# Attention-times-values product: from fp32 matmuls on half tiles to three fp32r matmuls on zero-padded full tiles

## The reference

```
x = x + 0.5 * F(layernorm(x))          # call 0
x = x + G(layernorm(x))                # middle stage, 16 heads, full attention
x = x + 0.5 * F(layernorm(x))          # call 1
```

```
h = shift_token(x)                     # second half of the features from the token before
q, k, v = split(h @ wqkv)              # 8 heads of 64
q, k = rotary(l2norm(q) * qs, l2norm(k) * ks)
o = local_attention(q, k, v)           # window 128: a block of 128 queries sees its own block and the one before
x = x + o @ wo
h = layernorm(shift_token(x)) * lg + lb
a, g = split(h @ w1 + b1)
x = x + (a * gelu(g)) @ w2 + b2
```

## Time and profile before

| | |
|---|---|
| median of 3 runs | 4246.81 us (4245.44 to 4254.26) |
| the profiled execution | 4246.81 us, span 4245.1 us |
| matmul engine busy | 3828.6 us, 90% |
| VectorE, ScalarE, GpSimd busy | 62%, 53%, 52% |
| call 0, middle stage, call 1 (roughly) | 44 to 1415, 1415 to 2790, 2790 to 4215 us |
| granted matmul clock, mean | 0.958 |

### The profile page before, as it was taken

The page is one execution under the profiler, slowest core; times in us unless marked ns, Lnnn a source line. Parts: engine busy times, 40 slices in busy tenths (PEclk is TensorE's granted clock), DMA queues, the critical chain, the costliest instruction groups (busy, mean ns, idle before and its releaser), DMA issues.

```text
span 4245.1 us, 75747 instructions
## 1 busy us (share of the span) xinstructions
PE 3828.6 (90%) x23552; PEld 3152.1 (74%) x23552; DVE 2628.4 (62%) x7288; ACT 2252.1 (53%) x5232; POOL 2197.2 (52%) x2175
## 2 busy tenths in 40 slices
PE   4898999899998879999999999968999998989987
PEld 3777777677777668888888888857777777777776
DVE  5666666666677455555555565546666665666764
ACT  2555665556655445454444544535556555566554
POOL 3455455545555345655555555635545554545652
PEclk9899999999999989999999999989999998999999
DMA  4000001110001010000000000010100011100000
GB/s 133 15 24 30 17 17 38 47 32 32 22 22 35 23 45 16 11 16 11 7 16 17 1 16 31 6 38 15 36 17 17 17 52 42 34 23 23 32 30 23
DMA packets 119072, 114.75 MB, mean 27 GB/s; under 512 B 13181, under 2 KB 116233, under 8 KB 118793
## 3 DMA queue, kind: packets, MB, share of 16 engines
q1 hardware_dynamic: 118792, 111.44, 8.1%
HBM read 73.69 MB, written 29.36 MB: 24 GB/s over the span
## 4 chain that ended last, share of the span: by engine, by line
PE 61%; DVE 15%; issue 9%; POOL 6%; ACT 5%; DMA 2%; SPq 1%; DVEq 0%; POOLq 0%; ACTq 0%
PE psum L1248 15%; PE psum L1249 14%; PE psum L1250 14%; PE psum L1350 5%; DVE probs L970 3%; PE psum L1360 3%; PE psum L1462 2%; ACT probs L713 2%; PE psum L1374 2%; PE psum L1339 2%; DVE nrm L1024 1%; POOL ge_lo L617 1%; PE psum L1392 1%; POOL probs L580 1%; PE psum L1442 1%
## 5 line engine op out<-in xcount | busy, mean ns | idle before, releaser
L617 POOL TENSOR_TENSOR ge_lo<-ge,ge_hi 128x512 fp32r<-128x512 f32 x512 | 722.7, 1415 | 527.9 <-DVE ge_hi L1137 283.1
L580 POOL TENSOR_SCALAR probs<-probs,rz 128x256 f32<-128x256 f32 (+1 forms) x1024 | 457.8, 466 | 653.7 <-DVE rz L984 653.7
L713 ACT ACTIVATE probs<-probs,nb,rq 128x256 f32<-128x256 f32 (+1 forms) x1024 | 575.8, 564 | 108.9 <-DVE nb L978 108.1
L801 ACT ACTIVATE ge<-psum 128x512 f32<-128x512 f32 x512 | 306.8, 599 | 611.8 <-PE psum L1462 579.1
L1137 DVE CAST ge_hi<-ge 128x512 fp32r<-128x512 f32 x512 | 249.3, 488 | 533.0 <-ACT ge L801 526.8
L970 DVE CUSTOM_DVE_ANT_0 probs<-psum,mask 128x256 f32<-128x256 f32 (+1 forms) x1024 | 339.5, 387 | 317.8 <-PE psum L1350 201.1
L570 POOL TENSOR_TENSOR rinv<-ssq,minus_half 128x16 f32<-128x16 f32 x128 | 377.0, 2946 | 119.5 <-DVE ssq L947 113.0
L1248 PE MATMUL psum<-wqkv_hi,hT_hi 128*128 128x512 f32 x768 | 341.7, 445 | 21.7 <-DVE turned_sin L936 15.2
L590 POOL TENSOR_TENSOR hid_lo<-gate,hid_hi 128x512 fp32r<-128x512 f32 x160 | 205.1, 1282 | 249.7 <-ACT hid_hi L744 249.7
L1350 PE MATMUL psum<-kT,qT 64*128 64x256 f32 (+1 forms) x2048 | 273.4, 386 | 67.6 <-DVE mx L970 45.0
L1249 PE MATMUL psum<-wqkv_hi,hT_lo 128*128 128x512 f32 x768 | 317.0, 413 | 0.0
(11 more groups left out here) (163 smaller groups left out, 10797.5 us busy)
## 6 DMA issues: line engine op xcount, KB each, us to landing
xnext<-stream SPq DMA_DIRECT2D x32, 512.0 KB, 4.3
xmid<-stream SPq DMA_DIRECT2D x32, 512.0 KB, 3.8
stream<-xmid SPq DMA_DIRECT2D x16, 512.0 KB, 2.9
nrm<-xmid SPq DMA_DIRECT2D x32, 224.0 KB
wbuf<-L_ffn_wqkv SPq DMA_DIRECT2D x8, 768.0 KB, 7.7
wbuf<-L_ffn_w SPq DMA_DIRECT2D x8, 682.0 KB, 5.6
x_all<-L_attn_x SPq DMA_DIRECT2D x8, 512.0 KB, 7.7
stream<-x_all SPq DMA_DIRECT2D x8, 512.0 KB, 3.9
```

What stands on the lines that cost most here:

```text
L580: last = nc.gpsimd.tensor_scalar(pu, pu, rz[:, h, t:t + 1], 1.0, ALU.mult, ALU.mult)
L617: nc.gpsimd.tensor_tensor(ges[1][:, k % 4, :], ge[:, k % 4, :], f32(ges[0][:, k % 4, :]), ALU.subtract).then_inc(S["g_lo"], 1)
L713: last = nc.scalar.activation(pu, pu, ACT.Exp, bias=nb[:, h, t:t + 1], scale=rq[:, 0, t, h:h + 1], accum_out=zs[:, h, t:t + 1])
L801: nc.scalar.activation(ge[:, k % 4, :], RB[k % 2], ACT.Exp, scale=GSCALE, accum_out=gz[:, h, t:t + 1]).then_inc(S["g_exp"], 1)
```

## The change

The values and the transposed weights are kept as fp32r pairs `hi` and `lo`, and the product goes through `three`.

- `v_s` replaces `vs`. For each pair of heads it has 192 columns: head 0, 64 zeros, head 1. The stationary operand of head 0 is columns 0 to 127 (head 0, zeros), that of head 1 columns 64 to 191 (zeros, head 1). Both heads write all 128 partitions of the bank and accumulate into it.
- ScalarE's vh writes the `hi` part. A new VectorE step `vl` writes the `lo` part, four times a round. It stands at four places of `DVE_STEPS`: vl0 between c1 and c2, vl1 between l and r, vl2 between r and the rotation rq3 that precedes the normalisation j, vl3 after the feed-forward multiplication of group 2.
- `bank_free` waits for vl where it waited for vh, and so does the first A of a round.
- H on ScalarE now copies both TB[0] and TB[1] to the `hi` part. L on VectorE waits for each copy and writes TB - hi to the `lo` part, for both sides. A waits for both L. The next T waits for L on both banks.
- GpSimd writes the zeros at the start of each call; the first A of a call waits for them.

```diff
@@ DVE_STEPS
-             "+rq0 L5 +ss0 R7 +rk0 -y5 L6 +rq1 +c0 +rk1 +ss1 -F -e L7 +ss2 +rq2 +rk2 P2 f0 P3 f1 +c1 +c2 x l r "
-             "+rq3 j +ss3 nl0 nl1 B +rk3 y0 f2 +c3 y1 +Y").split()
+            "+rq0 L5 +ss0 R7 +rk0 -y5 L6 +rq1 +c0 +rk1 +ss1 -F -e L7 +ss2 +rq2 +rk2 P2 f0 P3 f1 +c1 +vl0 +c2 x l "
+            "+vl1 r +vl2 +rq3 j +ss3 nl0 nl1 B +rk3 y0 f2 +vl3 +c3 y1 +Y").split()
@@ buffers
-    vs = sb("vs", [P, NT, INNER], c=ffn_mem)
-    pT = sb("pT", [P, 2, 2, 4 * P], c=ffn_mem)
+    v_s = [sb(f"v_{s}", [P, NT, PAIRS, 3 * DH], F32R, ffn_mem) for s in ("hi", "lo")]
+    pT = [sb(f"pT_{s}", [P, 2, 2, 4 * P], F32R, ffn_mem) for s in ("hi", "lo")]
@@ GpSimd, start of a call
-            pass
+            nc.gpsimd.memset(f32(v_s[0][:, :, :, DH:2 * DH]), 0.0)
+            nc.gpsimd.memset(f32(v_s[1][:, :, :, DH:2 * DH]), 0.0).then_inc(S["zeros"], 1)
@@ ScalarE, vh and H
-                    copy(vs[:, i, :], RB[(3 * i + 2) % 2]).then_inc(S["act_v"], 1)
+                    copy(v_s[0][:, i].rearrange("p a (s d) -> p a s d", s=3)[:, :, ::2, :],
+                         RB[(3 * i + 2) % 2].rearrange("p (a s d) -> p a s d", a=PAIRS, s=2)).then_inc(S["act_v"], 1)
...
-                    act.wait_ge(S["pe_p"], 2 * (UNITS * m + i) + 1)
-                    need(act, S["pe_av"], UNITS * m + i - 1)
-                    copy(pT[:, i % 2, 0, 0:w], TB[0][:, 0:w]).then_inc(S["act_p"], 1)
+                    for side in range(2):
+                        act.wait_ge(S["pe_p"], 2 * (UNITS * m + i) + side + 1)
+                        if side == 0:
+
+                            need(act, S["pe_av"], UNITS * m + i - 1)
+                        copy(pT[0][:, i % 2, side, 0:w], TB[side][:, 0:w]).then_inc(S["act_p"], 1)
@@ VectorE, vl and L
+                if kind == "vl":
+                    dve.wait_ge(S["act_v"], NT * m + i + 1)
+                    v3 = [v[:, i].rearrange("p a (s d) -> p a s d", s=3)[:, :, ::2, :] for v in v_s]
+                    V.tensor_tensor(v3[1], RB[(3 * i + 2) % 2].rearrange("p (a s d) -> p a s d", a=PAIRS, s=2),
+                                    f32(v3[0]), ALU.subtract).then_inc(S["dve_v"], 1)
...
-                    dve.wait_ge(S["pe_p"], 2 * (UNITS * m + i) + 2)
-                    need(dve, S["pe_av"], UNITS * m + i - 1)
-                    V.tensor_copy(pT[:, i % 2, 1, 0:w], TB[1][:, 0:w]).then_inc(S["dve_p"], 1)
+                    for side in range(2):
+                        dve.wait_ge(S["act_p"], 2 * (UNITS * m + i) + side + 1)
+                        V.tensor_tensor(pT[1][:, i % 2, side, 0:w], TB[side][:, 0:w], f32(pT[0][:, i % 2, side, 0:w]),
+                                        ALU.subtract).then_inc(S["dve_p"], 1)
@@ matmul engine, bank_free and A
-                need(pe, S["act_v"], NT * c + j + 1)
+                need(pe, S["dve_v"], NT * c + j + 1)
...
-                need(pe, S[("act_p", "dve_p")[side]], UNITS * c + j + 1)
+                need(pe, S["dve_p"], 2 * (UNITS * c + j) + side + 1)
...
-                        for side, h in enumerate(heads):
-                            last = mm(PAIR[p % 2][side * DH:(side + 1) * DH, t * P:(t + len(at)) * P],
-                                      vs[:, j, h * DH:(h + 1) * DH], pT[:, i % 2, side, at[0] * P:(at[-1] + 1) * P],
-                                      start=i % 2 == 0 and at[0] == 0, stop=i % 2 == 1 and at[-1] == len(cols) - 1,
-                                      skip_group_check=True)
+                    for side in range(2):
+                        for j in sorted({j for j, _ in cols}):
+                            at = [k for k, (j_, _) in enumerate(cols) if j_ == j]
+                            t = cols[at[0]][1]
+                            last = three(PAIR[p % 2][:, t * P:(t + len(at)) * P],
+                                         [v[:, j, p, side * DH:side * DH + P] for v in v_s],
+                                         [x_[:, i % 2, side, at[0] * P:(at[-1] + 1) * P] for x_ in pT],
+                                         i % 2 == 0 and side == 0 and at[0] == 0,
+                                         i % 2 == 1 and side == 1 and at[-1] == len(cols) - 1, skip_group_check=True)
```

More of the change, by code:

```diff
@@ L264, in build @@
     ACC = [psum[:, 6, :], psum[:, 7, :]]
-    names = """apart consts x0_out x0_stats x0_var x0_rs x0_z stage
+    names = """apart consts zeros x0_out x0_stats x0_var x0_rs x0_z stage
         w_in0 w_in1 w_hi w_lo w_small rope_ok bias_mm bias_ok
@@ L271, in build @@
         act_z act_sq act_sk act_v act_qt act_kt act_exp act_p act_av act_n act_gate act_u
-        dve_z dve_rq dve_rk dve_sum dve_ssq dve_k dve_scale dve_s dve_nb dve_rz dve_p dve_av dve_wo
+        dve_z dve_rq dve_rk dve_sum dve_ssq dve_k dve_v dve_scale dve_s dve_nb dve_rz dve_p dve_av dve_wo
         dve_st dve_mv dve_var dve_n dve_nlo dve_hid dve_old dve_w2
@@ L1366, in some_steps @@
                     if i == 0:
[L1367 to L1372, removed]
-                        for side, h in enumerate(heads):
-                            last = mm(PAIR[p % 2][side * DH:(side + 1) * DH, t * P:(t + len(at)) * P],
-                                      vs[:, j, h * DH:(h + 1) * DH], pT[:, i % 2, side, at[0] * P:(at[-1] + 1) * P],
-                                      start=i % 2 == 0 and at[0] == 0, stop=i % 2 == 1 and at[-1] == len(cols) - 1,
-                                      skip_group_check=True)
+                        pe.wait_ge(S["dve_v"], NT * (m + 1))
+                        if load is not None and load % LAYERS == 0:
+                            pe.wait_ge(S["zeros"], load // LAYERS + 1)
+                    pe.wait_ge(S["dve_p"], 2 * (UNITS * m + i) + 2)
+                    for side in range(2):
[7 more added lines that the diff above has]
+                                         i % 2 == 1 and side == 1 and at[-1] == len(cols) - 1, skip_group_check=True)
                     last.then_inc(S["pe_av"], 1)
```

## The result

The changed kernel takes 4352.24 us (4346.54 to 4355.29) against 4248.20 us for the kernel before, each the median of four runs: ratio 1.0242, 95% interval 1.0224 to 1.0260. It is 104 us slower. The direction was forecast; the size (4458 us, range from 4365) was not: the loss is half of what I expected.

A forecast was written before the change was run, and what follows sets the result against it. The matmul engine was taken to pace each round. Product 6.8, residual add 0.3, layernorm 0.68 and chain 0.3, less 1.5 swallowed waits, gave 6.6 us a round; 32 rounds, 211 us: 4458 us, own range 4380 to 4540, overall range 4365 to 4690.

The forecast's parts named there:

- The pace of the short matmul: Value product, matmul engine: each 128-column fp32r matmul takes 0.12 us, 72 a round, 8.64 us.
- fp32 pace: Rival for the value product: short fp32r matmuls take 0.22 us each, +14.0 us a round there, 4669 us; chance 0.24.
- columns alone: Rival for the value product: short matmuls take 0.065 us, only columns counting; 4.0 us a round, 4331 us; chance 0.05.
- The 81 ns of the Trainium skill: Guide's pace for 128-column load and matmul pairs; would make the short matmuls 5.8 instead of 8.64 us, time about 4368.
- Side by side: Value product: two heads' matmuls overlapped before, 7.28 us a round; full-width tiles prevent this, 14.4 us after.
- The product step "+6.8 us": Matmul engine, per round: new product 14.4 plus remaining switches 0.3, minus old product 7.28 and saved entries 0.6.
- switches of form: Matmul engine changing between fp32 and other work: 6 of 7 entries go, 0.6 us; two exits stay, 0.3 us.
- Swallowed waits: Matmul engine's waits for other engines in the two full stretches: the longer matmul queue absorbs 1.5 us a round.
- The other engines: Added copies and subtractions, per round: 0.3 us at the residual add, 0.68 before the layernorm's normalisation, 0.3 in the transpose-to-product chain.
- The clock: Rival: k3 inside the idle stretch before the layernorm's transposes stops the clock falling; 2.8 us a round back, 4368 us; chance 0.03.
- the two widths 0.12 us apart: Sign in the profile after: value-product matmuls of 256 and 128 columns both start 0.12 us apart.
- the round of 92 us: Sign in the profile after: the same step in neighbouring rounds starts some 92 us apart, against 85.27 before.

The follow-up runs named there:

- experiment 1: Kernel before with one added wait: key projection k3 may not start before VectorE has finished the layernorm's variance; 4212.58 us, ratio 0.9928.
- Experiment 4: Changed kernel with the product as fp32 matmuls on the zero-padded full-width tiles, hi parts only, all copies and subtractions kept; 4314.96 us, ratio 1.0162 to the kernel before.
- experiment 3: Changed kernel with the old fp32 half-tile product, heads side by side, hi parts only, all copies and subtractions kept; 4245.30 us, ratio 1.0003 to the kernel before.
- experiment 2: Changed kernel with the values' third subtraction (vl2) moved ahead of the layernorm's second statistics; 4365.61 us, ratio 1.0284 to the kernel before.
- 7: Value projection v3 moved ahead of the layernorm's transposes: kernel before 4204.11 us, the same with k3 also waiting for the variance 4207.48, changed kernel 4346.91.

## Why the prediction was wrong

With full clock from the transposes on, a round of the changed kernel takes 87.9 us, and one of the kernel before (experiment 1) 82.83: 5.1 us, where I had 6.6. Of this the clock takes back 1.0 to 1.1. In the six steady rounds the kernel before loses 84.63 - 82.83 = 1.8 us to it and the changed one 88.63 - 87.9 = 0.7; the 26 rounds give 1.0 at the steps n0 to g0. What is left, 4.0 us, is the measured difference of the six rounds.

- **The pace of the short matmul: right.** I took 0.12 us and it is 0.11 in a group. "fp32 pace" and "columns alone" both fall, although the time, 4352 us, landed near the 4331 of the latter; that is chance. The 81 ns of the Trainium skill ("TensorE: Matmul & The Clock Gate", "Back-to-back issue gap") is not seen either: in a row of short ones the starts are 0.11 us apart.
- **Side by side: right.** The product grows from 7.28 us (7.87 with the waits inside it) to 13.93, forecast 14.7. Experiment 4 shows the cause.
- **The product step "+6.8 us": the first step that failed, by size.** Its mechanism held. I had a net of 0.3 us for the switches of form (0.6 off, 0.3 left); 1.24 us went, and with the product's 0.8 the step was really 13.93 - 7.28 - 1.24 = 5.4. The forecast had 1.4 us a round too much. Experiment 4 bears out that it is the form: its fp32 product on full-width tiles takes 0.19 us off q2 and off W0 (1.57 and 1.62 us in experiment 3, 1.38 and 1.43 in 4), as the changed kernel does.
- **Swallowed waits: right in sum.** 1.5 forecast; 0.80 at w5 and 0.59 inside the old A steps, 1.39. The five waits of call 1 that vanished, 0.3 us a round, are in no term.
- **The other engines: nearly right in sum, wrong in place.** 0.3 + 0.68 + 0.3 = 1.28 forecast; nothing at the residual add, 0.49 at the layernorm, 0.55 at S4 and S6, 1.04.
- **The clock: the second step that failed, a term put at nothing.** I saw that k3 would move into the idle stretch, priced a kept clock at 2.8 us a round, and then gave it 3 in 100, as all or nothing, because one idle stretch of 2.43 us had also been followed by half clock. The price came from the round of the earlier trace rows, which has the long fall: that round loses 2.44 us, the mean one 1.8. And it was a middle case: the clock still fell in 26 of 30 rounds, but in 11 of them early enough to end inside the wait. The sum should have held 1.0 us for it, a little over a third of the price. The rival's 4368 us lies only 16 us from the result, but with 90 us for the clock where about 34 came; the product step makes up the difference by chance. Experiments 1, 2 and 7 show this term.

Between the forecast of 6.6 us a round and the 3.25 of the whole kernel lie 3.35: 1.4 from the product step, 1.0 to 1.1 from the clock, 0.3 from the five vanished waits, 0.1 from the two sums of smaller terms. The remaining half microsecond was not followed; most of it lies outside the 26 rounds, since these differ by 3.6 us. Of the signs that I had named, the two widths 0.12 us apart, units of 1.4 and 2.1 us and a product that waits little for the subtractions (20.8 us, 0.65 a round) came; the round of 92 us did not.

## What to carry to other kernels

Before widening a half tile with zeros, look whether two half-tile matmuls already run together: same count and duration with half the busy time is the sign. Giving that up made a product of 7.9 us a round 4.6 us longer here. Fp32r matmuls with a new stationary operand each took 0.11 us at 128 columns and 0.12 at 256, so halving the columns saved next to nothing. The idle stretch of the matmul engine cost twice here, once as such and once in the clock behind it; filling its middle with work that would have run anyway, even by adding a wait, made this kernel 0.7 to 1.0% faster. And where rounds alternate between two lengths, compare means over many rounds: the median of five, or two neighbouring rounds, put the clock's share at more than twice its size.

## What was not expected of the hardware

A pure delay shortened the program: 33 us from one added wait. The granted clock was 1.00 over a whole round with idle pieces of 1.78 and 2.26 us, and 0.98 over the next with the same pieces, so what follows such a pair is not settled by its lengths alone; a single piece of 4.25 us or more was followed by half clock every time in the kernel before and in that of experiment 2, sometimes for 3.4 us and sometimes for 6.8. Why one round keeps its clock and its neighbour does not stays open.

In a group of 256- and 128-column matmuls, the first short one is followed after 0.06 us, and the first long one behind short ones after 0.17 instead of 0.12.
